# A graph layer on one core: the node loop takes its tiles in groups of four in place of groups of three

## What is computed

```
h_self  = x @ W_self.T + b_self
h_neigh = segment_sum(x[src] @ W_neigh.T + b_neigh, dst)      # 100000 edges
out     = layernorm(x + relu(h_self + h_neigh))               # over the 128 features
```

## Time and profile before

| | us |
|---|---|
| median of 3 runs | 691.28 |
| lowest, highest | 684.82, 696.59 |
| time of the profiled execution | 693.77 |
| its span | 692.0 |
| PE busy in the span | 531.8 |
| POOL busy | 405.3 |
| DVE busy | 423.4 |
| ACT busy | 352.0 |
| mean granted TensorE clock | 0.88 |

### The profile page before, as it was taken

How to read it: one execution, slowest core, us unless ns; L and a number is a source line. 1 busy time by engine, 2 the same in 40 slices (tenths; PEclk the granted TensorE clock), 3 DMA queues, 4 the chain that set the end, 5 groups by cost and what they waited for, 6 DMA issues and landing times.

```text
span 692.0 us, 12704 instructions
## 1 busy us (share of the span) xinstructions
PE 531.8 (77%) x3281; PEld 468.0 (68%) x3281; DVE 423.4 (61%) x1919; ACT 352.0 (51%) x1049; POOL 405.3 (59%) x424
## 2 busy tenths in 40 slices
PE   2046187878899769778877988888987897789895
PEld 0035076767778758667766867777877787678794
DVE  7883267688867657867747664644554535555564
ACT  1010055456555454655654655565655556456686
POOL 4777566666666645766557656656556656565400
PEclk9999589899798878988989989997789799888998
DMA  2422134444444454454443544444444434444443
GB/s 78 123 59 56 53 89 134 113 122 136 126 121 133 132 151 118 123 135 128 128 121 103 162 126 125 129 129 123 120 121 131 128 110 133 134 134 128 126 127 85
DMA packets 122942, 82.20 MB, mean 119 GB/s; under 512 B 15374, under 2 KB 115894, under 8 KB 122840
## 3 DMA queue, kind: packets, MB, share of 16 engines
q1 hardware_dynamic: 109208, 53.63, 27.5%
q0 software_dynamic: 13664, 27.77, 15.4%
HBM read 55.44 MB, written 26.71 MB: 119 GB/s over the span
## 4 chain that ended last, share of the span: by engine, by line
PE 61%; issue 15%; DVE 9%; another core or an unknown queue 6%; ACT 5%; DMA 2%; ACTq 1%; SPq 1%; POOL 0%; DVEq 0%
PE bank L889 17%; PE bank L912 16%; PE bank L913 13%; PE bank L877 6%; PE bank L908 5%; PE bank L894 3%; ACT result L1023 2%; DVE pick L730 2%; DVE y L740 2%; ACT sums_t L996 2%; DMA x_in<-in_x 1%; DVE below L530 1%; DMA end_dst<-in_dst 1%; ACT std L1013 1%
## 5 line engine op out<-in xcount | busy, mean ns | idle before, releaser
L482 POOL DMA_INDIRECT ring<-in_x,chunk_src x391 | 380.9, 974 | 236.3 <-issue 87.6
L996 ACT COPY sums_t<-bank 128x192 f32 x391 | 124.6, 319 | 290.5 <-remote 109.4
L889 PE MATMUL bank<-pick,ring 128*128 128x193 f32 (+1 forms) x782 | 188.8, 367 | 42.2 <-DVE pick L730 17.4
L912 PE MATMUL bank<-wsum_t,x_t 128*128 128x128 f32 (+1 forms) x782 | 188.3, 328 | 0.0
L913 PE MATMUL bank<-wn_t,sums_t 128*128 128x128 f32 (+1 forms) x782 | 174.5, 310 | 1.0 <-issue 0.9
L889 PEld LDWEIGHTS bank<-pick,ring 128*128 128x128 f32 x782 | 141.3, 215 | 49.5 <-issue 29.0
L1023 ACT ACTIVATE result<-y,minus_mean,rstd 128x128 f32<-128x128 f32 x391 | 163.5, 486 | 0.0
L912 PEld LDWEIGHTS bank<-wsum_t,x_t 128*128 128x128 f32 (+1 forms) x782 | 138.1, 221 | 26.8 <-issue 26.7
L740 DVE SCALAR_TENSOR_TENSOR y<-bank,x_in 128x384 f32<-128x384 f32 x131 | 72.6, 554 | 134.2 <-PE bank L913 65.2
L913 PEld LDWEIGHTS bank<-wn_t,sums_t 128*128 128x128 f32 (+1 forms) x782 | 141.1, 225 | 0.3 <-issue 0.2
L730 DVE TENSOR_SCALAR pick<-columns,local 128x194 f32<-128x194 f32 x391 | 106.3, 328 | 0.2
(11 more groups left out here) (118 smaller groups left out, 195.8 us busy)
## 6 DMA issues: line engine op xcount, KB each, us to landing
x_in<-in_x SPq DMA_DIRECT2D x130, 192.0 KB
out<-result SPq DMA_DIRECT2D x130, 192.0 KB
ring<-in_x,chunk_src POOLq DMA_INDIRECT x391
degrees_t<-degrees_dram SPq DMA_DIRECT2D x130, 2.2 KB
dst_padded<-in_dst SPq DMA_DIRECT2D x1, 390.6 KB
src_padded<-in_src SPq DMA_DIRECT2D x1, 390.6 KB
edge_src<-in_src SPq DMA_DIRECT2D x1, 390.6 KB
edge_dst<-in_dst SPq DMA_DIRECT2D x1, 390.6 KB
```

Of the source, the lines that this page charges most:

```text
L482: nc.gpsimd.indirect_dma_start(ring[:, c % RING, :], None, x, bass.IndirectOffsetOnAxis(ap=chunk_src[:, c:c + 1], axis=0)).then_inc(gather ...
L889: ins = mm(into[:, frame:frame + SPAN + carried], ring[:, c % RING, :], pick[tau % DEEP][:, c % TRIO, 0:SPAN + carried], start=(c == 0), s ...
L912: mm(h, x_t[b][:, q, 0:rows], k.wsum_t[:], start=False, stop=False)
L996: nc.scalar.copy(sums_t[:, bass.ds(at, SPAN)], sum_bank[c // PAIR % SUM_BANKS][:, frame:frame + SPAN]).then_inc(sums_placed, 1)
```

## The change

Groups of four tiles (quads). The 391 tiles make 97 quads, one group of two tiles (388, 389) and one of the last tile alone (so that the last, of 80 rows, need not share a group): 99 steps in place of 131. All buffers of a group get four places; the ring stays at 24 chunks and the buffers at four groups. Each step now sums four chunks, as a rule. One instruction per group (L740, L776, L783, L908, L1004, L1013, the loads and stores) works on four tiles; instructions per tile or chunk stay as many. `first_tile` gives where a group starts. Two more bias loads stand ahead of the loop.

The list work is moved: the last two columns are packed with a whole bit (select and move) per step in steps 20 to 27 (before: half a bit in 21 to 36), started in step 19; their degrees take half a bit per step in steps 30 to 45 (before 39 to 54). The second column keeps its step numbers. SP stores the degrees of the last columns ahead of the loads of group 49 (before: group 66), and loads the edges ahead of those of group 28 (before 37).

```diff
-TRIO = 3
-TRIOS = -(-TILES // TRIO)
-FIRST_TRIOS = SPREAD // TRIO
+QUAD = 4
+FULL_QUADS = TILES // QUAD
+QUADS = FULL_QUADS + 2
 DEEP = 4
 PARTS = 3
-BIAS_ROWS = (TRIO + 1) * PARTS
+BIAS_ROWS = (QUAD + 1) * PARTS
...
+def first_tile(quad):
+    return TILES - 1 if quad == QUADS - 1 else min(TILES, QUAD * quad)
...
-def sums_needed(trio):
-    return chunks_starting_below(P * TRIO * (trio + 1))
+def sums_needed(quad):
+    return chunks_starting_below(P * first_tile(quad + 1))
...
     def tiles_of(tau):
-        return (1, LAST_ROWS) if tau == TRIOS - 1 else (TRIO, P)
+        if tau == QUADS - 1:
+            return 1, LAST_ROWS
+        return first_tile(tau + 1) - first_tile(tau), P
...
-            for q in range(TRIO):
+            for q in range(QUAD):
                 sp.dma_start(k.bias[q * PARTS:(q + 1) * PARTS, q, :], k.bias_part[:, :, 0, :]).then_inc(k.parts_landed, 16)
-                sp.dma_start(k.bias[TRIO * PARTS:BIAS_ROWS, q, :], k.bias_part[:, :, 1, :]).then_inc(k.parts_landed, 16)
+                sp.dma_start(k.bias[QUAD * PARTS:BIAS_ROWS, q, :], k.bias_part[:, :, 1, :]).then_inc(k.parts_landed, 16)
...
-            for tau in range(DEEP, TRIOS + DEEP + 2):
-                if tau == FIRST_TRIOS:
+            for tau in range(DEEP, QUADS + DEEP + 2):
+                if tau == SPREAD // QUAD:
                     store_degrees(2, 1, 2)
-                if tau == FIRST_TRIOS + DEEP:
+                if tau == SPREAD // QUAD + DEEP:
                     load_edges()
-                if tau == 2 * FIRST_TRIOS:
+                if tau == 2 * SPREAD // QUAD:
                     store_degrees(3, 2, COLUMNS)
...
-                if t == 20:
+                if t == 19:
                     pack_start(2, COLUMNS)
-                if 21 <= t < 37 and t % 2:
-                    shift_select(2, COLUMNS, (t - 21) // 2)
-                if 21 <= t < 37 and t % 2 == 0:
-                    shift_move(2, COLUMNS, (t - 21) // 2)
-                if t == 37:
+                if 20 <= t < 28:
+                    pack_bits(2, COLUMNS, [t - 20])
+                if t == 28:
                     pack_end(2, COLUMNS)
-                if t == 38:
+                if t == 29:
                     degrees_start(2, COLUMNS)
-                if t == 39:
+                if t == 30:
                     take_lists(3, 2, COLUMNS)
-                if 39 <= t < 55 and t % 2:
-                    shift_select(2, COLUMNS, (t - 39) // 2)
-                if 39 <= t < 55 and t % 2 == 0:
-                    shift_move(2, COLUMNS, (t - 39) // 2)
-                if t == 41:
+                if 30 <= t < 46 and t % 2 == 0:
+                    shift_select(2, COLUMNS, (t - 30) // 2)
+                if 30 <= t < 46 and t % 2:
+                    shift_move(2, COLUMNS, (t - 30) // 2)
+                if t == 32:
                     spread_lists(3, 2 * SPREAD, ENTRIES)
-                if t == 55:
+                if t == 45:
                     degrees_end(2, COLUMNS)
```

More of the change, by code:

```diff
@@ L111, in chunks_starting_below, with sums_ahead @@
     return 1 + max(c for c in range(CHUNKS) if P * c - drift_of(c) < node)
+def first_tile(quad):
+    return TILES - 1 if quad == QUADS - 1 else min(TILES, QUAD * quad)
 def whole_pairs(chunks):
     return min(CHUNKS, -(-chunks // PAIR) * PAIR)
-def sums_needed(trio):
-    return chunks_starting_below(P * TRIO * (trio + 1))
-def sums_ahead(trio):
-    return whole_pairs(sums_needed(min(trio, TRIOS - 1)) + PAIR)
+def sums_needed(quad):
+    return chunks_starting_below(P * first_tile(quad + 1))
+def sums_ahead(quad):
+    return whole_pairs(sums_needed(min(quad, QUADS - 1)) + PAIR)
 def lap_joined_after(lap):
@@ L166, in build_constants @@
     k.bias_part = sb("bias_part", [1, 3, 2, DIM], BF16)
-    k.bias = sb("bias", [BIAS_ROWS, TRIO, DIM], BF16)
+    k.bias = sb("bias", [BIAS_ROWS, QUAD, DIM], BF16)
     k.row0 = sb("row0", [P, P])
@@ L260, in build_common_case @@
     ring = sb("ring", [P, RING, DIM])
-    x_in = [sb(f"x_in{i}", [P, TRIO, DIM]) for i in range(DEEP)]
-    pick = [sb(f"pick{i}", [P, TRIO, SPAN + 2]) for i in range(DEEP)]
+    x_in = [sb(f"x_in{i}", [P, QUAD, DIM]) for i in range(DEEP)]
+    pick = [sb(f"pick{i}", [P, QUAD, SPAN + 2]) for i in range(DEEP)]
     sums_t = sb("sums_t", [P, LAP + MARGIN])
-    x_t = [sb(f"x_t{i}", [P, TRIO, P]) for i in range(2)]
+    x_t = [sb(f"x_t{i}", [P, QUAD, P]) for i in range(2)]
     degrees_t = [sb(f"degrees_t{i}", [BIAS_ROWS, P], BF16) for i in range(DEEP)]
[L266 to L272, removed]
+    y = [sb(f"y{i}", [P, QUAD, DIM]) for i in range(DEEP)]
+    stats = [sb(f"stats{i}", [P, QUAD, 6]) for i in range(DEEP)]
+    mean_var = [sb(f"mean_var{i}", [P, QUAD, 2]) for i in range(DEEP)]
+    std = [sb(f"std{i}", [P, QUAD]) for i in range(DEEP)]
+    rstd = [sb(f"rstd{i}", [P, QUAD]) for i in range(DEEP)]
+    minus_mean = [sb(f"minus_mean{i}", [P, QUAD]) for i in range(DEEP)]
+    result = [sb(f"result{i}", [P, QUAD, DIM]) for i in range(DEEP)]
     bank = [ctx.enter_context(nc.psum_tensor(f"bank{i}", [P, 512], FP32)) for i in range(8)]
@@ L420, in _ @@
             for i in range(DEEP):
-                sp.wait_ge(stored[i], 16 * len(range(i, TRIOS, DEEP)))
+                sp.wait_ge(stored[i], 16 * len(range(i, QUADS, DEEP)))
         @block_.gpsimd
@@ L475, in gather @@
             def gather(c):
[L477 to L478 removed]
+                tau = c // QUAD
+                if c % QUAD == 0 and tau >= GATHER_SEMS:
                     pool.wait_ge(gathered[tau % GATHER_SEMS], gathers_upto(tau - GATHER_SEMS))
@@ L837, in _ @@
             built = 3
-            for t in range(TRIOS + 2):
-                if 1 <= t <= TRIOS:
+            for t in range(QUADS + 2):
+                if 1 <= t <= QUADS:
                     residual(t - 1)
@@ L844, in _ @@
                     clear_lap(cleared_at[t - 1])
-                while built * TRIO < sums_ahead(t + 1):
+                while built * QUAD < sums_ahead(t + 1):
                     build_picks(built)
                     built += 1
-                if 1 <= t <= TRIOS:
+                if 1 <= t <= QUADS:
                     statistics(t - 1)
-                if 2 <= t < TRIOS + 2:
+                if 2 <= t < QUADS + 2:
                     invert(t - 2)
-                if 1 <= t <= TRIOS:
+                if 1 <= t <= QUADS:
                     aggregate(t - 1)
-                if 2 <= t < TRIOS + 2:
+                if 2 <= t < QUADS + 2:
                     scale_mean(t - 2)
@@ L888, in sum_chunk @@
                 carried = 1 - c % PAIR
-                ins = mm(into[:, frame:frame + SPAN + carried], ring[:, c % RING, :], pick[tau % DEEP][:, c % TRIO, 0:SPAN + carried],
+                ins = mm(into[:, frame:frame + SPAN + carried], ring[:, c % RING, :], pick[tau % DEEP][:, c % QUAD, 0:SPAN + carried],
                          start=(c == 0), stop=True, skip_group_check=True)
@@ L944, in _ @@
             pe.wait_ge(k.weights_copied, 3)
-            pe.wait_ge(k.parts_landed, 16 * 2 * TRIO)
+            pe.wait_ge(k.parts_landed, 16 * 2 * QUAD)
             turn_x(0)
             summed = 0
-            for t in range(TRIOS):
+            for t in range(QUADS):
                 later_lists(t)
@@ L1028, in _ @@
             placed = 0
-            for t in range(TRIOS + 3):
+            for t in range(QUADS + 3):
                 while placed < sums_ahead(t):
```

36 lines of the change are left out of this document (18 added, 18 removed).

## The result

The changed kernel takes 695.64 us (median of 18 runs, 690.88 to 701.86); the kernel before, in 18 runs beside it, 687.33 (682.65 to 696.59). The ratio is 1.0103, 95% interval 1.0074 to 1.0132. A ratio is taken over those runs of each kernel that lie within 1.5% of its fastest, so it can differ from the ratio of the medians over all runs. The time lies in the stated range of 668 to 708, which was wide enough for either sign.

A forecast was written before the change was run, and what follows sets the result against it. POOL's gathers, 1.5 us each with word of PE's matmuls late, were taken as the bound, not PE. Span 86.5 + 1 + 561 + 38.2 + 1 = 687.7 us; time 687.7 + 1.8 - 2.5 = 687 us; range 668 to 708.

The forecast's parts named there:

- the late word: Among the gathers, word of PE's finished matmuls reaches the other engines 2.4 us late, against 0.06 us behind them.
- reading of coincidence: That the gathers cause the lateness of PE's word was read from the trace, not shown by a removal.
- the term for late bursts: POOL's bursts begun late because PE had not summed in time: 18 us before, forecast to fall to 14.
- the rule: POOL's pace among the gathers: 1.50 us per gather and about 0.12 us more per burst; 547 us for quads.
- the other end: Late bursts on POOL grow to 24 us if a quad's wait is longer by its size.
- The cycle of four gives PE more slack: Reason for taking 14 us: 6.13 us for 4.5 us of PE's work, against 3.12 for 2.96.
- Tail: Time behind the last gather: 38.2 us, +2 for more tiles left to multiply, less 1 for PE.
- The start: Filling of the ring: 86.5 us, +1 us since PE can have four tiles multiplied at its end, not six.
- a sign of being wrong at the root: The prediction fails at its root if the ring filling ends elsewhere than 86 us.
- PE, DVE, ACT, SP: hidden: PE saves at most 6 us, covered but for 1 us in the tail; DVE, ACT and SP change nothing.
- Rival A: PE and its per-step waits set the pace; 22 us saved and the clock rises, about 664 us; chance 0.2.
- Rival B: Slower: each quad's products on PE wait for a chunk of their own step; bursts late, 721 us; chance 0.15.

The follow-up runs named there:

- condition of 690: Sessions in which the kernel before took 691 and 696 us, near the 687 of the result; the same program and inputs took 560 to 561 us in others.
- experiment 1: POOL's wait for the gathers of eight groups ago taken out: of the changed kernel (quads) 669.35 us, ratio 0.971; of the kernel before (trios) 688.61 us, 0.990.
- experiment 2: All gathers behind the 24th left out, with the waits belonging to them: kernel before (trios) 542.41 us, changed kernel (quads) 525.79 us.
- condition of 560: Three sessions in which the kernel before took 561, 561 and 560 us, with the same program and inputs.

## Why the prediction was wrong

**The bound, right.** POOL's gathers and the late word set the pace, not PE. Its "reading of coincidence" is now shown by removal, for the condition of 690.

**Gathers: the term for late bursts, 14 us, is the step that failed.** 92 waits came (forecast 90 to 95), but only 41 of 89 bursts were of four, where the sum had them all so; the count agrees partly by luck. And a cycle of four took 6.44 us (median), not 6.13. "If it goes with the number of hand-overs it falls by 32/131 to 14": what the bursts of after have above the rule is 23 us, near the 24 that was named as the other end, where before had 18.6. The reason given for that end ("if a quad's wait is longer by its size") is not the cause. The term is two terms. Of PE's lateness the quads left nothing: without the group's wait the cycle of four is 6.02, and the quads are 1.9% faster than trios without it (0.971/0.990; 2.8% by the medians of all runs). "The cycle of four gives PE more slack" was right and undersized. The second term was never in the sum: 55 bursts that begin at a quad's first gather, 0.5 us each. Its price stood in the trace of before (the 10 bursts that begin at a trio's first gather are 0.36 us late in the median, the others 0.0), and the code shows the wait; but I costed what the change adds and removes, and this wait was neither: the grouping moved it onto the path.

**The sum.** Forecast of the last gather: 87.5 + 561 = 648.5; measured 654.19. Tail 39.2 forecast, 39.4 measured. The start has 0.7 of these 5.7 us (88.22). That the filling ended elsewhere than at 86 was named as a sign of being wrong at the root; it moved by 1.7 us with two gathers more, and the fault lay elsewhere. From there to the last gather are 566.0 us, forecast 561: 355 gathers by the rule make 543, since the filling took in two more than before, and 23 lie above it. So the burst term was 9 us short, and a rule that had less to cover hid 4 of them. That the tail's sum came out does not show its parts, which nothing here separates. The rest of the miss is the base: before's median is 687.33 in 18 runs, 691.28 in the three that were shown. A forecast of 0.6% below it was, from that base, 683, and the result 695.6.

**PE, DVE, ACT, SP: hidden, right.** PE's 19 us, DVE's 11 and ACT's 8 less gave nothing. DVE waits 125.7/99 = 1.27 us a step for the deviation, so the packing had room on average, and the stretch with the packing is no slower than the rest (experiment 1).

**Rival A, wrong as a rival and half right in its number.** With PE as the bound the grouping is worth 16.6 us (experiment 2), near its 22, but in a kernel of 542 us. Its 664 us took 5 us more for a faster clock, for which the prediction gives no working. Its page rule (the Trainium skill, TensorE: Matmul & The Clock Gate, "HAM oscillation", that gaps let the clock fall) agrees with the traces: a granted clock of 0.88 in after, 0.93 without the group's wait, 1.00 in the window shown without gathers. But the clock did not come first: it rose when POOL's wait was taken out, with PE's work left as it was.

**Rival B, right in sign and wrong in mechanism.** The wait for chunks of the own step is in every quad kernel and doubles PE's idle before the bias matmul (experiment 1), and cycles of four take 6.02 us with it. It named 3 us waits in many cycles and a clock below 0.85; POOL's longest wait was 3.5 us, the mean 1.52, the clock 0.884.

**The version that beats both** in the condition of 690 is quads without the group's wait: 669.35 us, 2.9% below before and, across sessions, 3.8% below after. In the condition of 560 trios stay ahead, by 0.9 to 1.0%.

## What to carry to other kernels

Where an engine works in bursts, ask of each instruction that can begin one how many waits it carries, and whether the size of the groups, the depth of the ring and the step of the producer share a factor: then the same instruction, with the most waits, begins most bursts (here read from counts and code; no ring of another divisor was run). A wait that is always met already is not free there, since the wait that ends late can then stand as an instruction of its own; take it out where another wait implies it, or put it into the middle of a burst. And when a change groups work differently, cost also what it neither adds nor removes but moves to the head of a queue.

## What the runs showed of the hardware

- With indirect gathers running back to back, in the session of the result and two of the five others, the word of PE's matmuls reached DVE and POOL 2.4 us late at the places shown, and 0.04 us late at the one without gathers. In the other three sessions it came 0.04 us late at the place shown with gathers running. In the five sessions of the experiments the kernel before took 691 and 696 us where the word was late and 560 to 561 us where it was not, 19% less. What makes the difference wasn't found.
- A gather costs 1.50 us of the cycle whether it brings 128 or 64 rows of 512 bytes, where the word is late; where it is not, 1.28 and 1.26 us.
- A gather names one semaphore; a second wait becomes an instruction of its own. Behind it the gather starts 0.72 us after that instruction, in place of 0.12 us, and 0.78 us after DVE hears of the same word, in place of 0.28.
